# Sliding-window attention and a ternary feed-forward on one core: stage order and the attention's matmul layout are changed

## The chip, the cores and the metric

One core of one Trainium2 chip runs the whole program in one launch. The metric is the device time in microseconds (us). Engines: TensorE (PE, with its weight loads listed apart as PEld), VectorE (DVE), ScalarE (ACT), GpSimd (POOL) and SyncE (SP), which here only issues DMAs. Matmuls write PSUM: 8 banks of 512 fp32 columns on 128 partitions.

## The reference

```python
def ref(x, Wqkv, bqkv, Wout, bout, fast_b, w_fc, w_proj, u, v, gate):   # x: (1, 8192, 512) fp32
    xn = layernorm(x)
    q, k, v_ = split(xn @ Wqkv + bqkv)              # 16 heads of 32
    # a block of 128 queries sees its own block and both neighbours
    s = q @ kwin.T / sqrt(512);  s = where(|kpos - qpos| <= 128 and inside, s, -1e30)
    att = (softmax(s) @ vwin) @ Wout + bout
    h = bitlinear(xn, w_fc) + gate * (xn @ v.T @ fast_b.T @ u.T)        # 512 -> 2048
    ffn = bitlinear(relu(h) ** 2, w_proj)                               # 2048 -> 512, ternary weights
    return x + att + ffn
```

All is fp32. Both kernels reach that precision by splitting a value into a high part and a rest (`_hi`, `_lo`, type fp32r, which TensorE takes in one pass) and adding products of the parts.

## The kernel before, in words

`build` calls `attention`, which writes x + attention + bias to a DRAM buffer `partial`, and then `feed_forward`, which adds its result to `partial` and writes `out`. Each is a block of its own: one ends before the other begins. Every engine's order is written out by hand.

**Attention** (L192 to L1030) goes over 32 tiles of 256 tokens. A tile has 32 steps (`STEPS`), one for each pair of a head and a block of 128 queries. Four heads (32 channels each) make a chunk of 128 channels, so four chunks of 8 steps make a tile. A step:

- PE `scores` (L901): q and k are kept *stacked* in `stack`: 96 rows hold q_hi, q_lo, q_hi against k_hi, k_hi, k_lo, so one 96-row matmul gives the three products at once, 128 queries on partitions and 384 keys as columns. The stack is built by DMA from `qk_parts` (SP, `stack_qk`, L530: 12 DMAs of 64 KB a chunk).
- DVE `mask_scale_max` (L780) masks, scales and takes the row's maximum; ACT `exp` (L709) gives the probabilities in fp32.
- PE `transpose_probs` (L917): three 128x128 transposes turn them so that keys stand on partitions; ACT `pT_high` and DVE `pT_low` copy them out as two fp16 parts.
- PE `probs_times_values` (L938): for each of 3 key blocks two matmuls against `values`, which hold three bf16 parts of v and a column of ones. DVE `fold` (L807) adds the parts, POOL divides by the sum. The output goes back through PE ("riders", L923, 16 a tile with those of the next x) to be transposed.
- Between them on PE stand the *jobs* (`job_part`, L969), a quarter of one job in each step: q and k of a chunk (24 matmuls of 256 columns), v of a block and the output projection of a block (12 of 512 columns each). A tile has 4, 2 and 2 of them: 24 + 12 matmuls for each chunk.

**Feed-forward** (L1273) goes over 16 tiles of 512 tokens. `prepare_feed_forward` (L1037) quantises and transposes the weights. Then each of 16 steps of a tile has nine 512-column matmuls up and eight down; the next x is loaded, normalised and transposed beside them. PE is in order; SP loads x and `partial` and stores the result.

PE line numbers used below: L290 (project q, k), L300 (project v), L965 (project out), L913 (scores), L934 (transposes of the probabilities), L931 (riders), L954 and L956 (products with values), L188 (bias sum, fp32), L379 (first block's keys), L1225 (a scale spread by fp32 matmuls).

Of the kernel before, what the change touches and what calls it, by code (L numbers as in the profile page):

```python
# [32 lines left out]
VW = 1 + 3 * DH  # L33
# [9 lines left out]
def settle(eng, ticks):  # L43


    eng.sem_inc(ticks[eng.engine], 1)


def block_rows(dram, block):

    return dram[bass.ds(block * P, P), :]

# [13 lines left out]

def prepare_attention(nc, x, Wqkv, bqkv, Wout, bout, wqkv_hi, wqkv_lo, wout_hi, wout_lo, qk_bias, out_bias, ident,
                      minus_half, job_ps, xT_places):

    NX = len(xT_places)
    with ExitStack() as ctx:
        def sb(name, shape):  # L80
            return ctx.enter_context(nc.sbuf_tensor(name, shape, F32))

        def sem(name):
            return ctx.enter_context(nc.semaphore(name))

        stage = sb("w_stage", [P, DC, 3 * D])
        wout_raw = sb("wout_raw", [P, DC, D])
        v_bias = sb("v_bias", [P, DC])
        v_bias_wide = sb("v_bias_wide", [P, DC, P])
        bout_wide = sb("bout_wide", [P, D])  # L90
        x_in = sb("pro_x", [P, NX, D])
        bn = sb("pro_bn", [P, NX, 6])
        stats = sb("pro_stats", [P, NX, 4])
        bias_ps = ctx.enter_context(nc.psum_tensor("bias_ps", [P, D], F32))
        chunk_in = [sem(f"wqkv_chunk_in{k}") for k in range(DC)]
        wout_in, biases_in = sem("wout_in"), sem("biases_in")
        hi_done, lo_done = sem("w_hi_done"), sem("w_lo_done")
        wide_done, bias_summed = sem("v_bias_wide_done"), sem("bias_summed")
        zeroed, ident_done, half_set = sem("ident_zeroed"), sem("ident_done"), sem("pro_half_set")
        x_here = [sem(f"pro_x_here{b}") for b in range(NX)]  # L100
        ln_step = [sem(f"pro_ln_step{b}") for b in range(NX)]
        xn_done, x_turned, xT_hi_done, xT_done = (
            sem("pro_xn_done"), sem("pro_x_turned"), sem("pro_xT_hi_done"), sem("pro_xT_done"))
        block = ctx.enter_context(nc.Block())

        def four(ps):
            return ps.rearrange("p (c t) -> p c t", c=DC)

        @block.sync
        def _(sp):  # L110
            for b in range(NX):
                sp.dma_start(x_in[:, b, :], block_rows(x, b)).then_inc(x_here[b], 16)
            for k in range(DC):
                sp.dma_start(stage[:, k, :], Wqkv[k * P:(k + 1) * P, :]).then_inc(chunk_in[k], 16)
            sp.dma_start(wout_raw[:, :, :], Wout.rearrange("(c p) n -> p c n", p=P)).then_inc(wout_in, 16)

        @block.gpsimd
        def _(pool):
            identity_on_pool(pool, nc, ident, zeroed, ident_done)
            nc.gpsimd.memset(minus_half[:, :], -0.5).then_inc(half_set, 1)  # L120
            pool.wait_ge(half_set, 1)
            for b in range(NX):
                inverse_std(pool, nc, stats[:, b, :], minus_half, ln_step[b], 3)
            with nc.allow_non_contiguous_dma("a bias vector, once"):
                pool.dma_start(v_bias[:, :], bqkv[2 * D:3 * D].rearrange("(c p) -> p c", p=P)).then_inc(biases_in, 16)
                pool.dma_start(qk_bias[:, :], bqkv[0:2 * D].rearrange("(c p) -> p c", p=P)).then_inc(biases_in, 16)
# [67 lines left out]

# [1442 lines left out]
```

## Time and profile before

| | us |
|---|---|
| median of 3 runs (lowest, highest) | 2812.26 (2809.57, 2814.84) |
| the profiled execution: its own time | 2811.49 |
| its span, first to last instruction | 2809.7 |
| PE busy in the span | 2724.4 (97%) |
| mean granted clock | 0.985 of 2.4 GHz |

The profile is one execution. Starts of instructions are recorded; ends on PE are modelled, so the time that a matmul takes from its neighbours is the distance between two starts (the pitch), not its duration. `x3` in a row in order of time says that three equal instructions were merged. A granted clock of 1.00 is 2.4 GHz, 0.5 is 1.2 GHz.

### The profile page before, as it was taken

How to read it: one execution, taken by the hardware profiler on the slowest of the kernel's cores; microseconds unless marked ns; L12 is line 12 of the kernel's file. 1: busy time of each engine (PE TensorE's matmuls, PEld its weight loads, DVE VectorE, ACT ScalarE, POOL GpSimd, SP SyncE). 2: the span in 40 equal slices, each digit the busy share in tenths (PEclk: the TensorE clock that was granted, in tenths of full speed). 3: DMA queues.
4: the chain of work that ended last, by engine and by line, in shares of the span. 5: the costliest groups of instructions: out<-in, count | busy, mean ns of one | idle time of the engine just before them, and what ended most of it. 6: DMA issues, size and time to landing. Idle time of an engine off the chain costs nothing. (4 is left out here: it accounts for less than half of the span.)

```text
span 2809.7 us, 63144 instructions
## 1 busy us (share of the span) xinstructions
PE 2724.4 (97%) x20744; PEld 2393.8 (85%) x20744; DVE 2025.0 (72%) x5704; ACT 1713.7 (61%) x3745; POOL 640.1 (23%) x812
## 2 busy tenths in 40 slices
PE   6899999999999999999999976999999999999998
PEld 5899999999999999999999965888888888888887
DVE  4799999999999999999999966444444444444443
ACT  4678778787787877878778755333333333333332
POOL 3223333233332333333333220111111111111111
PEclk9999999999999999999999987999999999999999
DMA  3333333333333333333333333111111111111101
GB/s 113 92 97 92 99 95 97 96 91 99 96 92 100 94 98 96 94 97 94 99 96 95 98 90 135 44 50 49 45 49 45 49 45 45 45 45 45 45 30 45
DMA packets 176970, 219.39 MB, mean 78 GB/s; under 512 B 32112, under 2 KB 115280, under 8 KB 176192
## 3 DMA queue, kind: packets, MB, share of 16 engines
q1 hardware_dynamic: 175840, 215.31, 26.8%
q8 instruction: 142, 2.33, 0.4%
q0 software_dynamic: 864, 0.73, 0.1%
q14 instruction: 124, 1.02, 0.1%
HBM read 80.91 MB, written 33.55 MB: 41 GB/s over the span
## 5 line engine op out<-in xcount | busy, mean ns | idle before, releaser
L716 ACT ACTIVATE probs<-neg_scores,neg_max 128x384 f32<-128x384 f32 (+1 forms) x1024 | 631.0, 616 | 342.9 <-DVE neg_max L789 335.9
L789 DVE CUSTOM_DVE_ANT_0 neg_scores<-score_ps,mask 128x384 f32<-128x384 f32 (+1 forms) x1024 | 560.8, 548 | 106.0 <-PE score_ps L913 47.9
L1444 ACT ACTIVATE relu<-up_ps,fc_scale 128x512 f32<-128x512 f32 x256 | 176.4, 689 | 655.0 <-PE up_ps L1575 655.0
L800 DVE TENSOR_TENSOR pT_lo<-pT_ps,pT_hi 128x384 f16<-128x384 f32 (+1 forms) x1024 | 562.0, 549 | 13.1 <-ACT xT_hi L729 4.6
L1518 DVE SCALAR_TENSOR_TENSOR sq<-up_ps,relu 128x512 f32<-128x512 f32 x256 | 177.1, 692 | 533.3 <-ACT relu L1444 533.0
L934 PE MATMUL pT_ps<-ident,probs 128*128 128x128 f32 x3040 | 504.1, 274 | 16.7 <-ACT probs L716 13.5
L727 ACT CAST pT_hi<-pT_ps 128x384 f16<-128x384 f32 (+1 forms) x1024 | 470.0, 459 | 2.6 <-PE pT_ps L934 2.6
L913 PE MATMUL score_ps<-stack 96*128 96x128 f32 (+2 forms) x1536 | 447.2, 346 | 0.0
L934 PEld LDWEIGHTS pT_ps<-ident,probs 128*128 128x128 f32 x3040 | 364.4, 141 | 85.2 <-DVE oT_lo L804 13.1
L1585 PE MATMUL down_ps<-proj_T,sq_hi 128*128 128x512 f32 x1024 | 408.8, 399 | 0.3 <-DVE sq_lo L1501 0.2
L1587 PE MATMUL down_ps<-proj_T,sq_lo 128*128 128x512 f32 x1024 | 404.3, 395 | 0.0
L1571 PE MATMUL up_ps<-f_xT_hi,fc_T 128*128 128x512 f32 x1024 | 399.2, 390 | 1.4 <-DVE low L1489 1.4
L1573 PE MATMUL up_ps<-f_xT_lo,fc_T 128*128 128x512 f32 x1024 | 399.2, 390 | 0.0
L628 POOL TENSOR_TENSOR o_heads<-o_sum,o_rcp 128x128 f32<-128x128 f32 x256 | 102.8, 402 | 949.0 <-DVE o_sum L814 949.0
L290 PE MATMUL job_ps<-xT_hi,wqkv_hi 128*128 128x256 f32 x1024 | 295.2, 288 | 2.6 <-PEq L318 2.6
L954 PE MATMUL o_ps<-values,pT_hi 128*128 128x97 bf16 x3040 | 293.9, 207 | 0.5 <-DVE oT_lo L804 0.5
L290 PE MATMUL job_ps<-xT_hi,wqkv_lo 128*128 128x256 f32 x1024 | 288.2, 281 | 0.0
L290 PE MATMUL job_ps<-xT_lo,wqkv_hi 128*128 128x256 f32 x1024 | 287.6, 281 | 0.0
L956 PE MATMUL o_ps<-values,pT_lo 128*128 128x65 bf16 x3040 | 286.8, 193 | 0.0
L913 PEld LDWEIGHTS score_ps<-stack 96*128 96x128 f32 x1536 | 253.3, 192 | 0.1
L954 PEld LDWEIGHTS o_ps<-values,pT_hi 128*128 128x128 f16 x3040 | 250.3, 97 | 0.8 <-DVE oT_lo L804 0.6
L956 PEld LDWEIGHTS o_ps<-values,pT_lo 128*128 128x128 f16 x3040 | 237.6, 98 | 5.9
(165 smaller groups left out, 5189.4 us busy)
## 6 DMA issues: line engine op xcount, KB each, us to landing
stack<-qk_parts SPq DMA_DIRECT2D x1536, 64.0 KB, 2.1
x_in<-in_L_attn_x SPq DMA_DIRECT2D x64, 256.0 KB, 3.2
y<-in_L_attn_x SPq DMA_DIRECT2D x64, 256.0 KB, 2.8
partial<-y SPq DMA_DIRECT2D x64, 256.0 KB, 3.4
f_x_in<-in_L_attn_x SPq DMA_DIRECT2D x64, 256.0 KB, 2.7
part_in<-partial SPq DMA_DIRECT2D x64, 256.0 KB, 3.5
out<-f_y SPq DMA_DIRECT2D x64, 256.0 KB, 2.0
fc_in<-in_L_ffn_w_fc SPq DMA_DIRECT2D x16, 256.0 KB, 6.0
```

The source lines that it names most:

```text
L290: last = nc.tensor.matmul(out, w[:, k, col:col + P], a[:, k, par, :] if is_k else own_tokens(a, par, k), start=(n == 0), stop=(n == 3 * DC ...
L716: nc.scalar.activation(probs[:, r, cols], neg_scores[:, r, cols], ACT.Exp, bias=neg_max[:, s % 4:s % 4 + 1], scale=-1.0).then_inc(probs_do ...
L727: last = nc.scalar.copy(pT_hi[:, s % 4, cols], pT_ps[:, r, cols])
L789: nc.vector.tensor_tensor_reduce(out=neg_scores[:, r, cols], in0=score_ps[:, r, cols], in1=mask[:, cols], scale=-SCORE_SCALE, scalar=3e38, ...
L800: last = nc.vector.tensor_tensor(pT_lo[:, s % 4, cols], pT_ps[:, r, cols], pT_hi[:, s % 4, cols], ALU.subtract)
L913: last = nc.tensor.matmul(score_ps[:, s % 2, (w - b) * P:(w - b + count) * P], q_cols(par, c, h, b), keys[:, at:at + count * P], start=Tru ...
L934: last = nc.tensor.transpose(pT_ps[:, r, w * P:(w + 1) * P], probs[:, r, w * P:(w + 1) * P], ident[:, :])
L954: nc.tensor.matmul(o_ps[:, g % 2, col:col + VW], pT_hi[:, r, t], v, start=(w == w0), stop=False)
L956: last = nc.tensor.matmul(o_ps[:, g % 2, col:col + 1 + 2 * DH], pT_lo[:, r, t], v[:, 0:1 + 2 * DH], start=False, stop=(w == w1 - 1))
L1571: nc.tensor.matmul(up_ps[:, s % 2, :], fc_T[:, k, cols], xT_hi[:, par, k, :], start=(k == 0), stop=False)
L1585: nc.tensor.matmul(down_ps[:, b, :], sq_hi[:, s % 2, t], proj_T[:, s, :], start=(s == 0), stop=False)
L1587: last = nc.tensor.matmul(down_ps[:, b, :], sq_lo[:, s % 2, t], proj_T[:, s, :], start=False, stop=(s == FB - 1))
```

## The change

The feed-forward runs first. It takes the residual x in place of `partial` (`part_in <- x`) and writes `partial`; it also stores both parts of its transposed, normalised x to a new DRAM buffer `xT` (8 DMAs of 256 KB a tile of 512 tokens). Attention runs second, reads `xT` back (4 DMAs of 256 KB a tile of 256 tokens), adds `partial` and writes `out`. Its own layer norm, its transposes of x, the `stack` with its DMAs, the transposes of probabilities and outputs, and the fp16 and bf16 parts are gone.

Attention now goes by *slots*, 128 in all: one chunk of four heads of one tile of 256 queries (what 8 steps were). Heads use strips of the 128x128 array: `tile_position=(h * 32, 0)` puts a matmul with 32 rows on row strip h, `(0, h * 32)` one with 32 output columns on column strip h.

- `scores`: query-on-partition scores as before, but three matmuls of 32 rows for each head (hi·hi, lo·hi, hi·lo), the four heads one behind the other, each into its own PSUM bank. DVE takes from them only the maximum (`find_max`, 8 a slot). Where the keys wrap around in their ring of four blocks (every other tile), a run of 384 columns is cut in two.
- The maxima, as two fp32r parts in `shift_cols`, are turned by two matmuls (`turn_shift`) and copied by ACT to `shift_T`.
- `turned_scores` computes the scores a second time with keys on partitions, and adds minus the maximum (a matmul with `pick`) and the mask (16 bf16 matmuls on 32x32 tiles, `eye` by `turned_mask`) in PSUM. ACT takes the exponential straight into `pT`, fp32: 4 of 512 columns and 4 of 256 a slot.
- `probs_times_values`: fp32 matmuls, 32 output columns for each head, moving `pT`; once with the values and once with ones for the sums. DVE takes the reciprocal of 128x256 and multiplies.
- Banks: a ring of six (`RB`), 17 uses a slot, and two for the jobs and the products. The jobs are the same 24 + 12 matmuls a slot.

```diff
+def attention_stage(nc, Wqkv, bqkv, Wout, bout, xT_dram, partial, out):
+    RB = 6
+    USES = 4 * HC + 1
+            def scores(t, b):
+                ...
+                for w, key, count in key_runs(i, b):
+                    for pass_ in range(PASSES):
+                        q = q_lo if pass_ == 1 else q_hi
+                        keys = k_lo if pass_ == 2 else k_hi
+                        for h in range(HC):
+                            rows = slice(h * DH, (h + 1) * DH)
+                            last = nc.tensor.matmul(
+                                ring_ps[:, ring_bank(use + h), w * P:(w + count) * P], q[rows, c, place, :],
+                                keys[rows, c, key:key + count, :], start=(pass_ == 0), stop=(pass_ == PASSES - 1),
+                                tile_position=(h * DH, 0))
+            def turned_scores(t, edge):
+                ...
+                for h in range(HC):
+                    nc.tensor.matmul(ring_ps[:, ring_bank(use + h), cols], pick[rows, :], shift, start=True, stop=False,
+                                     tile_position=(h * DH, 0))
+                for h in range(HC):
+                    for g in range(HC):
+                        nc.tensor.matmul(strip[:, mask_places, :], eye[rows, :], turned_mask[rows, g, masks, :],
+                                         start=False, stop=False, tile_position=(h * DH, g * DH))
+                for key, out_cols, places in parts:
+                    for pass_ in range(PASSES):
+                        for h in range(HC):
+                            last = nc.tensor.matmul(
+                                ring_ps[:, ring_bank(use + h), out_cols], keys[rows, c, key, :], q[rows, c, places, :],
+                                start=False, stop=(key == parts[-1][0] and pass_ == PASSES - 1),
+                                tile_position=(h * DH, 0))
+            def probs_times_values(t):
+                ...
+                for sums in range(2):
+                    for n, (blk, cols, source) in enumerate(parts):    # 256, 256, 128, 128 columns
+                        for h in range(HC):
+                            v = ones[:, :] if sums else values[:, blk % VR, head * DH:(head + 1) * DH]
+                            last = nc.tensor.matmul(job_ps[strip, bank, out_], v, pT[:, t % 2, h, source],
+                                                    start=(n == 0), stop=(n == len(parts) - 1),
+                                                    tile_position=(0, h * DH))
+            for t in range(STEPS + 4):
+                if t < STEPS:
+                    scores(t, 0)
+                if 2 <= t < STEPS + 2:
+                    probs_times_values(t - 2)
+                run_a(t, 0)
+                if 1 <= t <= STEPS:
+                    turned_scores(t - 1, False)
+                run_a(t, 1)
+                if t < STEPS:
+                    scores(t, 1)
+                run_b(t, 0)
+                if 1 <= t <= STEPS:
+                    turned_scores(t - 1, True)
+                run_b(t, 1)
+                if t < STEPS:
+                    turn_shift(t)
...
+                nc.vector.reciprocal(o_rcp[:, :], job_ps[:, bank, T:2 * T]).then_inc(rcp_done, 1)
...
+                    nc.scalar.activation(pT[:, t % 2, h, 0:4 * P], ring_ps[:, bank, :], ACT.Exp,
+                                         scale=SCORE_SCALE).then_inc(exped, 1)
...
+            def store_xT(i, par):
+                for b in range(NB):
+                    sp.wait_ge(xT_done, NB * i + b + 1)
+                    for low, xT in enumerate((xT_hi, xT_lo)):
+                        sp.dma_start(xT_rows(xT_dram, NB * i + b, low),
+                                     xT[:, par, :, b * P:(b + 1) * P].bitcast(F32)).then_inc(xT_stored[b], 16)
...
             def xT_high(i, par, b):
                 act.wait_ge(x_turned, NB * i + b + 1)
+                wait(act, xT_stored[b], 32 * (i - 1))
...
 def prepare_attention(...):        # POOL now also builds pick, ones, eye and turned_mask
+                    nc.gpsimd.affine_select(out=raw_mask[rows, :, n, :], in_=raw_mask[rows, :, n, :],
+                                            compare_op=ALU.is_ge, fill=NEG, base=0,
+                                            pattern=[[-sign * DH, HC], [sign, P]], channel_multiplier=-sign
+                                            ).then_inc(consts_set, 1)
...
 def feed_forward(nc, x, partial, fast_b, w_fc, w_proj, u, v, gate, out):
+    xT_dram = nc.dram_tensor("xT", [2 * x.shape[0], x.shape[1]], F32, kind="Internal").ap()
+    feed_forward_stage(nc, x, fast_b, w_fc, w_proj, u, v, gate, xT_dram, partial)
+    attention_stage(nc, *HELD["attention"], xT_dram, partial, out)
```

## Rows read from the trace of the kernel before

**Rows 1.** the page, engines busy; then granted clock in 40 slices
```profile
PE 2724.4 (97%) x20744; PEld 2393.8 (85%) x20744; DVE 2025.0 (72%) x5704; ACT 1713.7 (61%) x3745; POOL 640.1 (23%) x812
...
PEclk9999999999999999999999987999999999999999
```

**Rows 2.** stretches: length, busy PE, PEld, DVE, ACT, POOL, clock, DMA share, GB/s
```profile
0.00:1668.00 1668.00, 1623.35 (x15833) 1499.76 (x15834) 1498.71 (x4690) 1281.24 (x3012) 511.84 (x673) 0.99 0.36 96
1668.00:1744.00 76.00, 43.87 (x202) 32.53 (x201) 45.59 (x123) 43.37 (x86) 8.43 (x15) 0.66 0.47 162
1744.00:2800.00 1056.00, 1055.73 (x4707) 860.58 (x4708) 478.23 (x887) 389.06 (x647) 114.91 (x120) 1.00 0.13 44
```

**Rows 3.** stretches within the attention: steady state, then its run-out
```profile
400.00:1600.00 1200.00, 1198.22 (x11858) 1111.73 (x11855) 1113.94 (x3493) 954.41 (x2250) 374.34 (x480) 1.00 0.36 96
1645.00:1660.00 15.00, 10.97 (x99) 9.13 (x96) 11.67 (x42) 9.25 (x24) 1.20 (x3) 0.82 0.16 55
```

**Rows 4.** groups, 400 to 1600 us: count, busy us, mean ns, idle before
```profile
L934 PE MATMUL pT_ps<-ident,probs 128*128 128x128 f32 x2295 | 376.6, 273 | 1.8 <-ACT probs L716 0.9
...
L954 PE MATMUL o_ps<-values,pT_hi 128*128 128x97 bf16 x2296 | 220.5, 207 | 0.0
...
L814 DVE TENSOR_REDUCE o_sum<-o_ps 128x128 f32<-128x384 f32 x192 | 101.0, 526 | 0.0
```

**Rows 5.** order of time, PE, 1000 to 1004 us: start, duration, instruction
```profile
999.75 0.28 PE L290 MATMUL job_ps<-xT_hi,wqkv_hi 128*128 128x256 f32 x1
999.87 0.28 PE L290 MATMUL job_ps<-xT_lo,wqkv_hi 128*128 128x256 f32 x1
...
1000.57 0.49 PE L934 MATMUL pT_ps<-ident,probs 128*128 128x128 f32 x3
1000.81 0.48 PE L913 MATMUL score_ps<-stack 96*128 96x128 f32 x2
...
1002.27 0.21 PE L954 MATMUL o_ps<-values,pT_hi 128*128 128x97 bf16 x1
...
1002.69 0.19 PE L956 MATMUL o_ps<-values,pT_lo 128*128 128x65 bf16 x1
1002.72 0.42 PE L913 MATMUL score_ps<-stack 96*128 96x256 f32 x2
1002.98 0.44 PE L300 MATMUL job_ps<-wqkv_hi,xT_hi 128*128 128x512 f32 x1
1003.26 0.40 PE L300 MATMUL job_ps<-wqkv_hi,xT_lo 128*128 128x512 f32 x1
1003.49 0.41 PE L300 MATMUL job_ps<-wqkv_lo,xT_hi 128*128 128x512 f32 x1
```

**Rows 6.** order of time, PE: the fp32 matmuls at L1225
```profile
1724.39 1.06 PE L1225 MATMUL scale_ps<-diagonal,ones 128*128 128x128 f32 x8
```

**Rows 7.** order of time, PEld: weight loads of fp32 matmuls
```profile
25.91 0.19 PEld L188 LDWEIGHTS bias_ps<-wout_raw,v_bias_wide 128*128 128x128 f32 x1 [0.38 <-issue]
26.34 0.19 PEld L188 LDWEIGHTS bias_ps<-wout_raw,v_bias_wide 128*128 128x128 f32 x1 [0.24 <-issue]
```

**Rows 8.** order of time, PEld: weight loads of 128-column fp32r matmuls
```profile
31.51 0.19 PEld L379 LDWEIGHTS job_ps<-xT_hi,wqkv_hi 128*128 128x128 f32 x1
31.62 0.19 PEld L379 LDWEIGHTS job_ps<-xT_lo,wqkv_hi 128*128 128x128 f32 x1
```

**Rows 9.** VectorE and ScalarE groups in 400 to 1600 us
```profile
L716 ACT ACTIVATE probs<-neg_scores,neg_max 128x384 f32<-128x384 f32 x766 | 474.7, 620 | 246.0 <-DVE neg_max L789 240.6
...
L789 DVE CUSTOM_DVE_ANT_0 neg_scores<-score_ps,mask 128x384 f32<-128x384 f32 x765 | 422.1, 552 | 74.0 <-PE score_ps L913 29.4 <-ACT probs L716 25.2 <-issue 0.8
...
L789 DVE DVE_READ_ACCUMULATOR2_ANT neg_max<- 128x1 f32 x765 | 63.1, 82 | 0.0
...
L813 DVE RECIPROCAL o_rcp<-o_ps 128x4 f32<-128x4 f32 x192 | 33.7, 176 | 2.3
```

**Rows 10.** VectorE groups in 1690 to 1730 us
```profile
L1137 DVE RECIPROCAL inv_scale<-scale 128x1 f32<-128x1 f32 x12 | 1.9, 156 | 0.0
```

More of the change, by code:

```diff
@@ L32 @@
 ROUND = 1.5 * 2.0 ** 23
-VW = 1 + 3 * DH
 def wait(eng, sem, value):
@@ L46, in settle, with xT_rows @@
     eng.sem_inc(ticks[eng.engine], 1)
+    eng.sem_inc(ticks[eng.engine], 1)
 def block_rows(dram, block):
     return dram[bass.ds(block * P, P), :]
+def xT_rows(dram, block, low):
+    return dram[bass.ds((2 * block + low) * P, P), :].rearrange("p (k t) -> p k t", k=DC)
 def identity_on_pool(pool, nc, ident, zeroed, ready):
@@ L1270, in _, with feed_forward_stage @@
                 nc.scalar.copy(low_out[:, n * D:(n + 1) * D], turn_ps[0:3 * DH, n, :]).then_inc(u_copied, 1)
-def feed_forward(nc, x, partial, fast_b, w_fc, w_proj, u, v, gate, out):
+def feed_forward_stage(nc, x, fast_b, w_fc, w_proj, u, v, gate, xT_dram, partial):
     F = w_fc.shape[0]
@@ L1334, in feed_forward @@
         stored = [sem(f"stored{b}") for b in range(NB)]
+        xT_stored = [sem(f"xT_stored{b}") for b in range(NB)]
         block = ctx.enter_context(nc.Block())
@@ L1370, in _ @@
                 sp.sem_inc(stored[b], 16)
+            def store_xT(i, par):
+                for b in range(NB):
+                    sp.wait_ge(xT_done, NB * i + b + 1)
+                    settle(sp, ticks)
+                    for low, xT in enumerate((xT_hi, xT_lo)):
+                        sp.dma_start(xT_rows(xT_dram, NB * i + b, low),
+                                     xT[:, par, :, b * P:(b + 1) * P].bitcast(F32)).then_inc(xT_stored[b], 16)
+            store_xT(0, 0)
             def tile(i, par):
@@ L1378, in tile @@
                         settle(sp, ticks)
-                        sp.dma_start(block_rows(out, NB * (i - 1) + b), y[:, b, :]).then_inc(stored[b], 16)
+                        sp.dma_start(block_rows(partial, NB * (i - 1) + b), y[:, b, :]).then_inc(stored[b], 16)
                 for b in range(NB):
-                    sp.dma_start(part_in[:, b, :], block_rows(partial, NB * i + b)).then_inc(part_here[b], 16)
+                    sp.dma_start(part_in[:, b, :], block_rows(x, NB * i + b)).then_inc(part_here[b], 16)
+                if not is_last(i):
+                    store_xT(i + 1, 1 - par)
             tiles(sp, tile)
@@ L1385, in _ @@
                 sp.wait_ge(y_done, NB * (NT - 1) + b + 1)
-                sp.dma_start(block_rows(out, NB * (NT - 1) + b), y[:, b, :]).then_inc(stored[b], 16)
+                sp.dma_start(block_rows(partial, NB * (NT - 1) + b), y[:, b, :]).then_inc(stored[b], 16)
             for b in range(NB):
                 sp.wait_ge(stored[b], 16 * (NT + 1))
+                sp.wait_ge(xT_stored[b], 32 * NT)
         @block.gpsimd
@@ L1613, with attention, feed_forward @@
+HELD = {}
+def attention(nc, x, Wqkv, bqkv, Wout, bout, partial):
+    HELD["attention"] = (Wqkv, bqkv, Wout, bout)
+def feed_forward(nc, x, partial, fast_b, w_fc, w_proj, u, v, gate, out):
+    xT_dram = nc.dram_tensor("xT", [2 * x.shape[0], x.shape[1]], F32, kind="Internal").ap()
+    feed_forward_stage(nc, x, fast_b, w_fc, w_proj, u, v, gate, xT_dram, partial)
+    attention_stage(nc, *HELD["attention"], xT_dram, partial, out)
 _INS = ["L0_attn_x", "L0_attn_Wqkv", "L0_attn_bqkv", "L0_attn_Wout", "L0_attn_bout", "L0_ffn_fast_b", "L0_ffn_w_fc",
```

1372 lines of the change are left out of this document (578 added, 794 removed).

## The prediction

> **What bounds the kernel now.** I read the page's busy line first, then the stretches, then TensorE's rows in order of time. PE is busy 97% of the span and its clock is at its upper level nearly throughout [rows 1]. The attention takes 1668 us, the feed-forward's preparation and first transposes 76 us, its steady part 1056 us with PE never idle [rows 2]. In the attention's steady part PE is busy for 1198 of 1200 us, DVE for 1114 [rows 3]; the transposes, PE's first to wait for anybody, wait 1.8 us in all [rows 4]. DVE's fold L814 runs 192 times there, 8 a tile, so 24 tiles: 50.0 us a tile, **12.5 us a slot** (a chunk of four heads, 8 steps). PE's order sets the end in both stages, and the change is worth what it does to PE's 12.5 us.
>
> What fills them, by pitches [rows 5]: the q and k matmuls follow at 0.12 (24 a slot: 2.8 us), the 512-column ones at 0.23 (12: 2.8 us), the three transposes of a step take 0.24 (24 and 4 riders: 2.3 us), twelve value products 0.45 (48: 1.8 us), a step's score matmuls 0.26 (2.1 us). Sum 11.8; 0.7 us are handovers.
>
> **What stays.** The feed-forward's PE order is the same. New there are 8 stores of xT a tile of 66 us, 2 MB or 32 GB/s beside the 44 that it moves now, while the attention moves 96 [rows 2]: hidden, on SP's queue behind loads that are one tile early; were they late, the wait would be ACT's copy of a tile two back. Cost 0 (bounds 0 and 10 us). The attention's preparation loses layer norm and gains some 25 small POOL operations beside the same weight loads; its first slot still waits for 36 + 24 + 48 matmuls, and x now comes from DRAM. Its run-out stands at the kernel's end and the feed-forward's before the attention. I set all of this to 0, bounds -10 and +30 us. So T = 2811.5 (the profiled execution, 0.8 under the median) + 128 x (new slot - 12.5).
>
> **The jobs** are the same: 5.6 us a slot.
>
> **What goes:** stacked scores, transposes, riders, bf16 products, 6.2 us a slot, and DVE's and ACT's copies, which were beside PE anyway.
>
> **What comes, on PE.** No row of the trace has strips of the array, so each term is bounded from both sides: all strips at once, or one after the other.
>
> 1. *Products with values and ones.* An fp32 matmul is two records: the four at L1225 are x8 in the trace [rows 6]. A record takes 0.43 us for 512 columns [rows 7], two cycles of 2.4 GHz a column, and 0.11 us for 128, from (1.06 - 0.27) / 7 [rows 6]. So a 256-column head product is 2 x 0.21 = 0.43 us. A slot has 2 x (256 + 256 + 128 + 128) columns for each of four heads: 2.6 us if four strips run at once, 10.2 us if none do. I take **5.1**: matmuls start in program order [rows 5], and the two records of one head stand next to each other on the same strip. The second must wait for the first, and the next head's first starts behind it. Only a second record and the next head's first can overlap, so half of the serial cost stays.
> 2. *Row-strip groups of four heads.* Scores: two directions x 3 passes of 384 columns, or 256 and 128 where keys wrap: 6 or 12 groups, 9 on average. Turned scores: 7 groups (one of 512, six of 256), then 7 (one of 256, six of 128). At 0.457 ns a column (0.117/256) and a weight load of 128 columns at 0.11 [rows 8] as the floor of each strip, all at once is 1.2 + 0.9 + 0.8 = 2.9 us. But each group is four load-and-matmul pairs, and the fastest pairs in the trace come at 0.038 us (eleven from 1002.27 to 1002.69 [rows 5], of 97 and 65 columns), 0.15 a group: 1.4 + 1.1 + 1.0 = **3.5**, which I take. If loads of different strips don't overlap, 92 loads x 0.11 = 10.1 us; with nothing overlapping 11.
> 3. *Masks.* 32 small bf16 matmuls of 256 columns: 0.2 us all at once, 3.7 one by one; at the issue pitch 32 x 0.038 = **1.2**.
> 4. *Turning the maxima:* 2 x 0.11 = **0.2**.
>
> Sum: 5.6 + 5.1 + 3.5 + 1.2 + 0.2 = **15.6 us a slot**, 3.1 more than now.
>
> **The other engines** don't reach that. DVE: 8 maxima x (0.55 + 0.08) = 5.0; a reciprocal costs 156 ns at one column and 176 at four [rows 9, 10], 6.7 ns a column, so 1.9 us for 256; the rest (product 0.4, q and k rests 1.0, the split 0.4, half an output 0.3) makes 9.0. ACT: eight exponentials, 4 x 0.73 + 4 x 0.51 (0.62 at 384 columns [rows 9]), and some 2 us of copies: 7. PE waits for ring banks: the turned scores need two of the four banks just scored, 1.3 us of DVE, behind 5.1 us of products; the second scores need two exponentials, 1.5 us, behind 1.4 us of job. Such waits cost tenths at most: 0, upper bound 0.5 us a slot. Queued behind a waiting matmul is all of PE, the jobs too; here a pause of 0.5 us meets DVE and ACT with half of their time free.
>
> The sum is 128 x 3.1 = 397 us: **3210 us**.
>
> **A rule that would add to it.** By the Trainium skill (TensorEngine Tiling (Array Packing), Key Properties) "changing tiling mode (not just tile) drains the TensorE". In this trace nothing shows it: the 97-column products follow transposes and 96-row scores follow them without a gap of over 0.1 us [rows 5]. My sum goes without it.
>
> **Rivals.**
> - *Strips really run four at once, issue costs nothing* (0.20): 5.6 + 2.6 + 2.9 + 0.4 + 0.2 = 11.7 us, **2710**. For it: PE's whole argument is then columns, and a 384-column group hides its issue. Against it: the two records of an fp32 product must start out of order. The skill (TensorE: Matmul & The Clock Gate, Packing small matmuls) says that matmuls on different strips start about 4 ns apart, and also that they start in strict order; the first half would give this case, both together my forecast.
> - *Four at once for the fp32 products, pairs at 0.038* (0.10): 13.1 us, **2890**: slower still.
> - *Each change of strip shape drains PE* (0.13): a slot changes shape some 13 times (scores, products, job, turned scores around the masks, job, and so on). A drain is the part of a matmul behind its pitch, 0.40 - 0.23 = 0.17 us [rows 5]: 2.2 us a slot, **3490**. This is what the rule above would do.
> - *Weight loads of different row strips go one by one* (0.13): 5.6 + 5.1 + 10.1 + 1.2 + 0.2 = 22.2 us, **4050**. For it: loads are the floor of a 128-column matmul now [rows 8]. Against it: a strip's load touches other rows of the array.
> - *No overlap at all, so that strips don't do what they say* (0.04): 5.6 + 10.2 + 11 + 3.7 + 0.2 = 30.7, **5140**.
>
> My forecast has 0.40. The faster case turns on one point: with everything else ideal the slot is 9.1 + products, so products must cost under 3.4 us, which half overlap (5.1) excludes.
>
> A clock at the lower level is no case of its own: in the run-out PE was busy 11 of 15 us and the clock 0.82 [rows 3], but a PE-bound slot has no such pauses.
>
> **Range.** The forecast's own is 3050 to 3350 (a third less or all of the bank waits, issue at 0.025 to 0.04). With the rivals at 2710, 2890 and 3490 the range is 2690 to 3700; 4050 and 5140 (0.17) are left out. Executions agree within 0.2%, so that is what can be told from no change: faster 0.21, within 0.2% 0.01, slower 0.78.
>
> **What would show it.** The jobs' pitches unchanged at 0.12 and 0.23. For the products: starts of four heads' records; 1.71 us for four heads at 256 columns is serial, 0.85 to 1.07 my half, 0.43 full overlap. For the row strips: the time from one pass's first head to the next pass's, 0.15 to 0.18, against 0.44 for serial loads. Stretches of the feed-forward as before. PE near 100% busy in the attention, DVE near 60%, ACT near 45%. Wrong it would be if the products of a slot took under 3.4 us, if PE waited for DVE's maxima or for exponentials by over 0.5 us a slot, or if the granted clock fell in the steady part.

## The result, and the profile after

The changed kernel takes 2987.8 us (median; 2986.8 to 2991.4) against 2813.6 us for the kernel before on the same chip: a ratio of 1.063, 95% interval 1.061 to 1.064. I had forecast 3210 us. Slower it is, by 174 us where I had said 397.

The page after, busy engines and the granted clock, beside [rows 1]:

```profile
PE 2899.6 (97%) x33680; PEld 2280.8 (76%) x33680; DVE 1512.4 (51%) x3905; ACT 1068.2 (36%) x2341; POOL 325.7 (11%) x367
...
PEclk6999999999999996999999999999999999999999
```

TensorE is as busy as before (97%), with 1.6 times as many matmul records (33680 for 20744). The stretches of the changed kernel: feed-forward's preparation, its steady part, the attention's preparation in two pieces, and the attention in steady state (columns as in [rows 2]):

```profile
0.00:76.00 76.00, 47.32 (x205) 35.89 (x206) 46.28 (x124) 44.80 (x87) 6.44 (x17) 0.69 0.53 182
76.00:1132.00 1056.00, 1052.50 (x4693) 857.60 (x4691) 478.23 (x890) 387.65 (x646) 117.22 (x123) 1.00 0.24 74
1132.00:1160.00 28.00, 6.59 (x32) 1.38 (x32) 8.61 (x6) 7.78 (x5) 22.60 (x37) 0.53 0.55 193
1160.00:1190.00 30.00, 16.59 (x70) 15.49 (x71) 3.06 (x6) 1.73 (x5) 2.66 (x1) 0.54 0.44 123
...
1300.00:2700.00 1400.00, 1394.71 (x22644) 1078.11 (x22644) 766.57 (x2251) 492.16 (x1250) 138.21 (x150) 1.00 0.13 40
```

The edges of these stretches are chosen, not found. From the first to the last matmul of the feed-forward's tiles it is 1058.6 us, where it was 1057.2, now with 74 GB/s where it had 44 [rows 2]: its eight stores a tile are hidden. Its preparation, up to that first matmul, takes 69.8 us from the start of the span; before, it took 72.4 us from the attention's last matmul. In the attention's steady part PE is busy for 1394.7 of 1400 us at a granted clock of 1.00. VectorE, which stood at 93% [rows 3], is at 55%. So what has grown is the work on TensorE itself. The slot is read from VectorE's reciprocal, one a slot; the row gives count, shortest, median and longest in ns, and first and last start:

```profile
L1135 DVE RECIPROCAL o_rcp<-job_ps x128: 1756/1758/1759, 1218.2 to 2977.7; 128x256 f32<-128x256 f32 x128
```

(2977.7 - 1218.2) / 127 = **13.85 us a slot**, against 12.5. 128 x 1.35 = 173 us, of the 180 us between the two profiled spans (2989.6 and 2809.7). The other 7 lie outside the slots, in the preparations and the run-out, which I had set to 0.

One slot in order of time on PE (start, duration, instruction). xcount is what the view puts in one row; x4 is the four heads of a row-strip pass:

```profile
2000.87 0.28 PE L1203 MATMUL job_ps<-xT_hi,wqkv_lo 128*128 128x256 f32 x1
2001.07 0.51 PE L1300 MATMUL ring_ps<-shift_T,pick 32*128 32x512 f32 x4
2001.51 0.33 PE L1306 MATMUL ring_ps<-turned_mask,eye 32*32 32x256 bf16 x16
2001.77 0.39 PE L1314 MATMUL ring_ps<-q_hi,k_hi 32*128 32x256 f32 x4
2001.99 0.29 PE L1314 MATMUL ring_ps<-q_lo,k_hi 32*128 32x256 f32 x4
2002.11 0.29 PE L1314 MATMUL ring_ps<-q_hi,k_lo 32*128 32x256 f32 x4
...
2002.47 0.28 PE L1314 MATMUL ring_ps<-q_hi,k_lo 32*128 32x256 f32 x4
2002.68 0.39 PE L1203 MATMUL job_ps<-xT_hi,wqkv_hi 128*128 128x256 f32 x1
2002.90 0.28 PE L1203 MATMUL job_ps<-xT_lo,wqkv_hi 128*128 128x256 f32 x1
2003.02 0.28 PE L1203 MATMUL job_ps<-xT_hi,wqkv_lo 128*128 128x256 f32 x1
...
2010.56 0.28 PE L1270 MATMUL ring_ps<-k_lo,q_hi 32*128 32x128 f32 x4
2010.77 1.51 PE L1351 MATMUL job_ps<-pT,values 128*32 128x256 f32 x32
2012.09 1.48 PE L1351 MATMUL job_ps<-pT,ones_strip 128*32 128x256 f32 x32
2013.51 0.38 PE L1203 MATMUL job_ps<-xT_hi,wqkv_hi 128*128 128x256 f32 x1
```

What to see there:

- The jobs' pitches are unchanged: 0.12 us (2002.90 to 2003.02).
- *Products.* 32 records with values and 32 with ones, from 2010.77 to 2013.51: 2.74 us. Four heads' first records start 7 ns apart (2010.767, .774, .781, .787), their second ones 0.24 us later: all four strips run at once.
- *Row strips.* A pass of four heads takes 0.12 us (2001.99 to 2002.11), as long as one matmul of 256 columns on the whole array.
- *Edges.* Wherever the tile shape changes, the distance is too long. The last 256-column job matmul is followed after 0.20 us (2000.87 to 2001.07) where 0.12 is its pitch. The maxima's 512 columns, pitch 0.23, take 0.44 until the masks. The masks take 0.26 where a job matmul of as many columns takes 0.12, the first pass of turned scores 0.22 (2001.77 to 2001.99), the last one 0.21 (2002.47 to 2002.68), and the first job matmul behind it 0.22. Each change of shape costs about 0.1 us on the last group ahead of it and 0.1 on the first behind it, and there are 13 a slot. A change of operands in one shape costs nothing: the last output job is followed by the turning of the maxima, also on the whole array, after 0.24 us (2009.43 to 2009.67), its pitch being 0.23.
- *Weight loads at an edge.* Within a shape a load starts ahead of its own matmul, 0.12 us here (2000.75 for the matmul at 2000.87). Across a change it starts only together with it (2001.07 for 2001.07). In the 1400 us, no load starts between the last matmul before a change and the first behind it in 1275 of 1300 changes.

```profile
2000.75 0.19 PEld L1203 LDWEIGHTS job_ps<-xT_hi,wqkv_lo 128*128 128x128 f32 x1
2001.07 0.19 PEld L1300 LDWEIGHTS ring_ps<-shift_T,pick 32*128 32x128 f32 x4
```

VectorE and ScalarE in steady state, beside my prices of 0.55, 0.73 and 1.9 us; the idle time in front of them shows that they wait for PE, and not the other way:

```profile
L1116 DVE CUSTOM_DVE_ANT_0 masked_scores<-ring_ps,mask 128x384 bf16<-128x384 f32 x800 | 398.3, 554 | 473.2 <-PE ring_ps L1270 473.2
...
L1051 ACT ACTIVATE pT<-ring_ps 128x512 f32<-128x512 f32 x400 | 206.6, 604 | 626.9 <-PE ring_ps L1314 626.9
L1135 DVE RECIPROCAL o_rcp<-job_ps 128x256 f32<-128x256 f32 x101 | 177.5, 1758 | 82.7 <-PE job_ps L1351 82.7
```

PE's own waits in the same 1400 us are this one row:

```profile
PE job_ps L1351 <- issue: 5.3, 25, 0.3
```

### The profile page after: what moved, and what is told of

Read it like the earlier page. It is cut to its first block, busy times and chain, and to the rows that moved or that the text cites. A ratio compares the mean times of both kernels' runs of the same rounds, so it can differ in the third digit from the quotient of the medians.

```text
span 2989.6 us, 79871 instructions
## 1 busy us (share of the span) xinstructions
PE 2899.6 (97%) x33680; PEld 2280.8 (76%) x33680; DVE 1512.4 (51%) x3905; ACT 1068.2 (36%) x2341; POOL 325.7 (11%) x367
## 4 chain that ended last, share of the span: by engine, by line
PE 60%; issue 0%; DVE 0%; ACT 0%; DMA 0%; SPq 0%; POOL 0%; POOLq 0%; ACTq 0%
PE job_ps L1203 14%; PE job_ps L1351 12%; PE ring_ps L1314 7%; PE job_ps L1212 7%; PE ring_ps L1270 7%; PE job_ps L1223 7%; PE ring_ps L1300 3%; PE ring_ps L1306 2%; PE ring_ps L1327 1%; PE job_ps L1363 0%; DMA xT_lo<-xT 0%; SPq L984 0%; DVE masked_scores L1116 0%; ACT pT L1051 0%; DVE o_rcp L1135 0%
## 5 line engine op out<-in xcount | busy, mean ns | idle before, releaser
L1116 DVE CUSTOM_DVE_ANT_0 masked_scores<-ring_ps,mask 128x384 bf16<-128x384 f32 (+1 forms) x1024 | 505.5, 550 | 599.0 <-PE ring_ps L1270 599.0
L1051 ACT ACTIVATE pT<-ring_ps 128x512 f32<-128x512 f32 x512 | 264.4, 604 | 794.2 <-PE ring_ps L1314 794.2
L1135 DVE RECIPROCAL o_rcp<-job_ps 128x256 f32<-128x256 f32 x128 | 225.0, 1758 | 112.2 <-PE job_ps L1351 112.2
L623 PEld LDWEIGHTS up_ps<-f_xT_hi,fc_T 128*128 128x128 f32 x1024 | 192.8, 188 | 44.2 <-DVE low L541 2.2
L637 PEld LDWEIGHTS down_ps<-proj_T,sq_hi 128*128 128x128 f32 x1024 | 193.4, 189 | 42.8 <-DVE sq_lo L553 1.1
L639 PEld LDWEIGHTS down_ps<-proj_T,sq_lo 128*128 128x128 f32 x1024 | 193.0, 188 | 43.1
L625 PEld LDWEIGHTS up_ps<-f_xT_lo,fc_T 128*128 128x128 f32 x1024 | 192.8, 188 | 42.6
L1351 PE MATMUL job_ps<-pT,values 128*32 128x256 f32 (+1 forms) x4032 | 193.0, 332 | 6.6 <-issue 6.6
L1203 PEld LDWEIGHTS job_ps<-xT_hi,wqkv_lo 128*128 128x128 f32 x1024 | 193.0, 188 | 0.0
L1203 PEld LDWEIGHTS job_ps<-xT_lo,wqkv_hi 128*128 128x128 f32 x1024 | 192.8, 188 | 0.1
```

The source lines that it names most:

```text
L623: nc.tensor.matmul(up_ps[:, s % 2, :], fc_T[:, k, cols], xT_hi[:, par, k, :], start=(k == 0), stop=False)
L625: nc.tensor.matmul(up_ps[:, s % 2, :], fc_T[:, k, cols], xT_lo[:, par, k, :], start=False, stop=False)
L637: nc.tensor.matmul(down_ps[:, b, :], sq_hi[:, s % 2, t], proj_T[:, s, :], start=(s == 0), stop=False)
L639: last = nc.tensor.matmul(down_ps[:, b, :], sq_lo[:, s % 2, t], proj_T[:, s, :], start=False, stop=(s == FB - 1))
L1051: nc.scalar.activation(pT[:, t % 2, h, 0:4 * P], ring_ps[:, bank, :], ACT.Exp, scale=SCORE_SCALE).then_inc(exped, 1)
L1116: nc.vector.tensor_tensor_reduce(out=masked_scores[:, b * HC + h, cols], in0=ring_ps[:, bank, cols], in1=mask[:, cols], scale=-1.0, scalar ...
```

## Experiments

All are edits of the changed kernel. A slot's time is read from the reciprocal's starts, as above. The kernels ran on four chips; each ratio is to the kernel before on the same chip, which took 2811 us (2809 for the last kernel). The diffs are shortened, some to lines in words.

### The order of the heads in the products

```diff
-for sums in range(2):
-    for n, (blk, cols, source) in enumerate(parts):
-        for h in range(HC):
+for sums in range(2):
+    for h in range(HC):
+        for n, (blk, cols, source) in enumerate(parts):
```

The wait for the edge exponentials, which stood ahead of the third key block, now stands ahead of all the products. It isn't the cause of what follows: PE's waits come to 3.8 us in 1400, against 5.3 before the edit.

> The value and ones products take the heads in the outer loop and the key blocks in the inner one: the same matmuls, but all of one strip stand next to each other. Theory A (matmuls start strictly in program order, and one whose strip is busy holds up every later one): the four strips no longer run at once, the products go from 2.7 us a slot to between 8 and 10.2, +5.5 to +7.5 us a slot, so 3690 to 3950 us. Theory B (each strip has work of its own waiting, and a later strip's matmul passes one whose strip is busy): nothing changes, 2988 us within 15. Theory C (it can look ahead, but only over a few matmuls): in between; a strip has 8 records in a row there. The slot's period and the starts of the four heads' records show which.

Measured: 3599 us, ratio 1.280 (1.278 to 1.282), 18.66 us a slot, +4.80. PE in order of time:

```profile
1999.83 1.60 PE L1350 MATMUL job_ps<-pT,values 128*32 128x256 f32 x11
2001.16 0.40 PE L1350 MATMUL job_ps<-pT,ones_strip 128*32 128x256 f32 x1
2001.27 0.38 PE L1350 MATMUL job_ps<-pT,values 128*32 128x128 f32 x2
2001.40 0.38 PE L1350 MATMUL job_ps<-pT,ones_strip 128*32 128x256 f32 x1
...
2001.62 3.71 PE L1350 MATMUL job_ps<-pT,ones_strip 128*32 128x256 f32 x30
```

Products with ones of one head stand among products with values of another (2001.16 to 2001.62): strips do overlap, but late. The block takes 7.5 us instead of 2.74. The starts of the records, read one by one (columns: start, column count):

```
head 0:  2016.303 256   .543 256   .759 256   .975 256   2017.191 128   .300 128   .409 128   .518 128
head 1:  2017.196 256   .436 256   .652 256   .868 256   2018.084 128   ...
head 2:  2018.090 256   ...
```

Head 1 begins 5 ns after head 0's fifth record of eight starts, head 2 again 6 ns after head 1's fifth. So it looks as if three records of a strip can wait behind the one that starts, and the matmuls of other strips pass them, while a further one holds up everything behind it in program order. Eight such blocks: 7 offsets of 0.89 us are 6.25, and the last block 1.30: 7.55, as measured. Neither theory A nor theory B but C.

### The same for the row strips

```diff
-for w, key, count in key_runs(i, b):
-    for pass_ in range(PASSES):
-        for h in range(HC):
+for h in range(HC):
+    for w, key, count in key_runs(i, b):
+        for pass_ in range(PASSES):
```

(and likewise in `turned_scores`.)

> Same edit for the row strips: heads outside, passes inside, in the scores of both directions and in the turned scores. The slot has 21 groups of four matmuls that take 2.9 us when the four strips run at once. Theory A (in program order, a busy strip holds up all): up to four times that less the overlap of the ends, +5 to +8 us a slot, 3630 to 4000 us. Theory B (a strip's matmul passes one that waits for another strip): 2988 us within 15. Theory C (look-ahead over a few only): in between. The bank of head 0 is then finished earlier than the others; maxima and exponentials are beside PE anyway, so that is worth 0.

Measured: 3347 us, ratio 1.191 (1.189 to 1.193), 16.62 us a slot, +2.77. The turned scores of a main block in order of time, three matmuls of the first head, and then a row that merges the second head's first (2008.163) with the first head's fourth (2008.276):

```profile
2007.82 0.38 PE L1314 MATMUL ring_ps<-q_hi,k_hi 32*128 32x256 f32 x1
2008.04 0.28 PE L1314 MATMUL ring_ps<-q_lo,k_hi 32*128 32x256 f32 x1
2008.16 0.28 PE L1314 MATMUL ring_ps<-q_hi,k_lo 32*128 32x256 f32 x1
2008.16 0.39 PE L1314 MATMUL ring_ps<-q_hi,k_hi 32*128 32x256 f32 x2
```

A head has six records here. The next head's first starts 6 ns after the third (2008.157 and 2008.163): again three are left waiting, and a matmul starts ahead of one that stands before it in program order. Where a head has three records, as in the scores whose keys don't wrap, all four heads start within 30 ns (2054.305 to 2054.335), and the order of the heads costs next to nothing: the group takes 0.75 us to the next one, against 0.73. That is why the price is 2.77 us and not theory A's 5 to 8. Two kinds of matmul, fp32 in column strips and fp32r in row strips, give the same number, three records.

### Two matmuls a head before the next head

```diff
-for n, (blk, cols, source) in enumerate(parts):
-    for h in range(HC):
+for pair in range(0, len(parts), 2):
+    for h, n in ((h, n) for h in range(HC) for n in range(pair, min(pair + 2, len(parts)))):
+        blk, cols, source = parts[n]
```

> Between the changed kernel and the one with the heads outermost: the products take the key blocks two at a time, so each head issues two fp32 matmuls (four records) before the next head's. Theory R (a strip takes a few records ahead: the records of the heads-outer kernels show the next head's first starting 6 ns after the strip before it has three records left, fp32 or fp32r; matmuls are handed out in program order into that room): four records fit, so nothing changes, 2988 us within 10. Theory M (room for one record behind the running one): each pair of matmuls delays the next strip by two records of 0.216 us, +1.2 us for each of the four pairs of 256 or 128 columns together about +3.5 us a slot, 3430. What I had predicted (no room at all) would make it slower still.

Measured: 2997 us, ratio 1.066 (1.065 to 1.068), 13.93 us a slot: +0.08, where theory M asked for 3.5. Four records fit. The values pass takes 1.33 us, in the changed kernel 1.32:

```profile
2011.44 1.54 PE L1352 MATMUL job_ps<-pT,values 128*32 128x256 f32 x32
2012.77 1.55 PE L1352 MATMUL job_ps<-pT,ones_strip 128*32 128x256 f32 x32
```

The four heads' first records are now 13 ns apart instead of 7 (2011.441 to 2011.481). When the fourth head starts, three records of each of the other three are waiting, nine in all. So the room is each strip's own, and not one of three for all strips together, which the kernel with the heads outermost in the products can't tell apart.

### Is the overlap real, and is TensorE the bound?

```diff
-for sums in range(2):
+for sums in (0, 1, 1):
```

> The products with ones are done twice (the second pass overwrites the first with the same sums): 16 fp32 matmuls more a slot, 32 records. Theory F (four strips at once, and TensorE is the bound): the 12 records of the values pass took 1.37 us, so +1.33 to +1.37 us a slot, +170 to +175 us, 3160. Theory H (my half overlap, hidden somewhere in the trace): +2.55 us a slot, +326 us, 3314. Theory W (a wait for VectorE or ScalarE fills part of the slot): less than +100 us.

Measured: 3156 us, ratio 1.122 (1.121 to 1.124), 15.19 us a slot, +1.33. Theory F; half overlap would have given twice that. (A pass has 32 records, not the 12 of the expectation.) The 64 records with ones take 2.74 us, 1.37 a pass:

```profile
2006.08 1.51 PE L1351 MATMUL job_ps<-pT,values 128*32 128x256 f32 x32 [0.27 <-issue]
2007.38 2.81 PE L1351 MATMUL job_ps<-pT,ones_strip 128*32 128x256 f32 x64
2010.12 0.39 PE L1203 MATMUL job_ps<-xT_hi,wqkv_hi 128*128 128x256 f32 x1
```

### More changes of shape

```diff
-for h in range(HC): masks of head h
-turned scores, passes 1 to 6
+for h in range(2): masks of head h
+turned scores, pass 1
+for h in range(2, 4): masks of head h
+turned scores, passes 2 to 6
```

> The 16 mask matmuls before the turned scores are done in two batches of eight, with the first pass of the turned scores (four row-strip matmuls) between them: the same instructions in another order. It adds two changes of tile shape to each of the two turned-score groups, four to a slot. Theory D (each change of shape drains TensorE; 0.195 us a change, from the stretched distances in the changed kernel's trace): +0.78 us a slot, +100 us, 3088 (within 25). Theory N (no price on a change; the 1.2 us a slot that my accounting lacks lie elsewhere, in issue for example): 2988 within 10.

Measured: 3091 us, ratio 1.100 (1.098 to 1.101), 14.63 us a slot, +0.77. The instructions are the same: theory D. Each group has its own two edges now:

```profile
2001.54 0.30 PE L1307 MATMUL ring_ps<-turned_mask,eye 32*32 32x256 bf16 x8
2001.77 0.39 PE L1316 MATMUL ring_ps<-q_hi,k_hi 32*128 32x256 f32 x4
2002.09 0.30 PE L1307 MATMUL ring_ps<-turned_mask,eye 32*32 32x256 bf16 x8
2002.32 0.39 PE L1316 MATMUL ring_ps<-q_lo,k_hi 32*128 32x256 f32 x4
2002.54 0.28 PE L1316 MATMUL ring_ps<-q_hi,k_lo 32*128 32x256 f32 x4
```

Eight masks take 0.23 us (2001.54 to 2001.77), and sixteen took 0.26: a group of masks costs its two edges and hardly its matmuls. Pass 1 between the masks takes 0.32 (2001.77 to 2002.09), with a change on both sides, and pass 2 0.22, with one behind it; without any it is 0.12.

### Fewer changes of shape

Edge masks ahead of the maxima, so that the maxima and the turned scores stand together:

```diff
-nc.tensor.matmul(ring_ps[...], pick[rows, :], shift, start=True, ...)
+if edge: masks_of(True)                 # the masks open the bank
+nc.tensor.matmul(ring_ps[...], pick[rows, :], shift, start=not edge, ...)
+if not edge: masks_of(False)
```

> In the turned scores of the edge blocks the masks come ahead of the matmuls that add the maxima, so that those stand next to the turned scores, which have the same shape: job, masks, maxima, turned scores instead of job, maxima, masks, maxima's shape again. One change of tile shape fewer a slot, same instructions. Theory D (0.195 us a change): -25 us, 2963 (within 8). Theory N: 2988 within 4.

Measured: 2961 us, ratio 1.054 (1.052 to 1.055), 13.64 us a slot, -0.22. On top of it, the q and k job in one piece:

```diff
-run_a(t, 0)
 if 1 <= t <= STEPS: turned_scores(t - 1, False)
+run_a(t, 0)
 run_a(t, 1)
```

> On top of the kernel with the edge masks first: the turned scores of the main blocks come straight after the products and before the q and k job, whose two halves then stand together. The same instructions, two changes of tile shape fewer (job to maxima, turned scores to job). Theory D: -0.39 us a slot, 2961 - 50 = 2911. Rival: the turned scores now need the maxima of two of the four banks just scored, with only the products between; if those take longer than the products' 2.7 us, TensorE waits and the gain is lost, 2950 to 3000.

Measured: 2940 us, ratio 1.046 (1.044 to 1.047), 13.47 us a slot, -0.17. I had miscounted: products, job, maxima become products, maxima, so one change goes, not two; for one change theory D asks for -0.2. PE didn't wait for the maxima. And on top of that, the main masks last:

```diff
-if not edge: masks_of(False)
 for key, out_cols, places in parts: ...      # turned scores
+if not edge: last = masks_of(False)
```

> On top of the kernel with the jobs together (2940 us; my count of its changes was wrong: it saves one, not two, since the products then meet the row strips directly; it has 11 a slot against 12 and 13): the masks of the main blocks come last in their group, between the turned scores and the job, so that the maxima and the turned scores, which have one shape, stand together. Same instructions, 10 changes a slot. Theory D, at the 0.17 to 0.21 us that the last two removals gave: 2913 to 2919. Theory N: 2940.

Measured: 2913 us, ratio 1.036 (1.035 to 1.038), 13.31 us a slot, -0.16. Five kernels with the same instructions now stand in one line:

| changes of shape a slot | us a slot | time, us |
|---|---|---|
| 17 | 14.63 | 3091 |
| 13 (the changed kernel) | 13.85 | 2988 |
| 12 | 13.64 | 2961 |
| 11 | 13.47 | 2940 |
| 10 | 13.31 | 2913 |

The slope is (14.63 - 13.31) / 7 = **0.19 us a change**. By that slope, carried on below the 10 that were tried, 13 of them are an estimated 2.5 us a slot, 316 us, more than the 174 us that the changed kernel lost, and without them the slot would take 11.4 us.

### Fewer columns

What I tried next is in the products. The three key blocks' probabilities are added before the sum over keys is taken, so that one matmul of 256 columns a head replaces four. First with GpSimd doing both adds, on the kernel with 12 changes:

```diff
+nc.gpsimd.tensor_tensor(p_sum, pT[main block 0], pT[main block 1], ALU.add)
+nc.gpsimd.tensor_tensor(p_sum[edge cols], p_sum[edge cols], pT[edge cols], ALU.add)
-ones products of all four parts
+nc.tensor.matmul(job_ps[strip, bank, T:2 * T], ones, p_sum[:, t % 2, h, :], start=True, stop=True, ...)
```

> The kernel with the edge masks first, and the probabilities of the three key blocks added beforehand, both adds on GpSimd; the one ones product a head stands behind the turned scores of the main blocks, some 4 us after the value products. By pitches: -0.94 us a slot of products, and one change of tile shape more (turned scores, sums, job in place of turned scores, job), +0.2: 2961 - 120 + 25 = 2866. Rival: GpSimd's two adds of 1024 columns (2.4 us each in the last profile) end too late and TensorE waits: 2900 to 2960.

Measured: 2881 us, ratio 1.024 (1.022 to 1.026), 13.02 us a slot: -0.62 against the 12-change kernel, where the sum said -0.74. Then with the jobs together, the sums next to the value products, and VectorE adding the edges (11 changes):

> What the measurements point to, all at once: edge masks first; jobs together; and the sums from probabilities added beforehand over the three key blocks (GpSimd adds the two main blocks, VectorE the edge ones), so that one fp32 matmul of 256 columns a head replaces four, next to the value products. By the pitches: -27 (measured), -50 (two changes), -0.94 us a slot for 1.37 - 0.43 us of ones products, -120: 2791 us, 0.7% below the kernel before. Rival: the sums come late (GpSimd 2.5 us for 1024 columns by its 1.28 us for 512, then VectorE behind the edge exponentials), TensorE waits in front of them, and the 120 us are lost in part: 2820 to 2900, slower than before.

Measured: 2847 us, ratio 1.013 (1.012 to 1.015), 12.73 us a slot. The 2791 had my miscount in it; by the kernel with 11 changes it is 13.47 - 0.94 = 12.53. Of the missing 0.2 us about 0.1 is in my 0.94, which is 1.37 - 0.43: the group of ones products, from its first start to the next group's, goes from 1.41 us (11 changes, old sums) to 0.55 where nothing waits, since its edge stays, and that is 0.86. The other 0.1 is a wait, though not the rival's: the same distance is 0.65 us here on average. PE's waits in the 1400 us, PE between the ones products and the maxima, and VectorE ahead of that:

```profile
PE ring_ps L1330 <- DVE neg_max L1127: 5.2, 27, 0.2
...
2006.50 0.61 PE L1386 MATMUL job_ps<-p_sum,ones_strip 128*32 128x256 f32 x8
2007.18 0.51 PE L1330 MATMUL ring_ps<-shift_T,pick 32*128 32x512 f32 x4
```

```profile
2004.87 1.22 DVE L1176 TENSOR_TENSOR p_sum<-p_sum,pT 128x1024 f32<-128x1024 f32 x1
2006.00 0.55 DVE L1127 CUSTOM_DVE_ANT_0 masked_scores<-ring_ps,mask 128x384 bf16<-128x384 f32 x1
...
2006.95 0.08 DVE L1127 DVE_READ_ACCUMULATOR2_ANT neg_max<- 128x1 f32 x1
```

The ones products start in time (2006.50, behind 1.33 us of values). But the edge add, 1.22 us, stands in front of VectorE's maxima, whose second one frees the second bank at 2007.03; the maxima's matmuls start at 2007.18. With the add shared between VectorE and GpSimd, and the main masks last (ten changes):

```diff
-dve: p_sum[:, 0:4, edge] += pT[:, 0:4, edge]
+dve: p_sum[:, 0:2, edge] += pT[:, 0:2, edge]
+pool: p_sum[:, 2:4, edge] += pT[:, 2:4, edge]
```

> The last combination (2847 us), with the main masks last as well, and the edge add shared: VectorE adds the edge probabilities of two heads, GpSimd those of the other two. Ten changes a slot. In the last profile TensorE stood 0.25 us in front of the maxima's matmuls, waiting for VectorE's second maximum, behind its add of 1.22 us; with half of the add that goes, -0.2 us a slot, 25 us. The change of shape gives 25 more: 2797 (within 12), 0.5% below the kernel before. Rival: GpSimd's half, 1.2 us behind the last exponential and slowed by VectorE, is late for the ones products instead: 2810 to 2830, no better than before.

Measured: 2815 us, ratio 1.0009 (1.0000 to 1.0018), 12.44 us a slot; by 13.31 - 0.94 it would be 12.37, with 0.86 it is 12.45. Level with the kernel before. One of PE's waits is left, once in four slots; the two rows of ScalarE and the one of PE show where it is:

```profile
PE job_ps L1389 <- issue: 6.0, 28, 0.3
```

```profile
2012.63 0.37 ACT L1058 CAST shift_T<-ring_ps 128x256 fp32r<-128x256 f32 x1 [0.55 <-PE ring_ps L1365]
2012.90 0.59 ACT L1064 COPY values<-job_ps 128x512 f32<-128x512 f32 x1
```

```profile
2013.59 0.64 PE L1389 MATMUL job_ps<-pT,values 128*32 128x256 f32 x8 [0.16 <-issue]
```

The first product of a new tile needs the v block that ScalarE copies at 2012.90, behind the turned maxima's copy at 2012.63. Turning these two round:

```diff
-copy_shift(t - 1)
 if b and b[0] == "v": take_v(...)
+copy_shift(t - 1)
```

> The ten-change kernel (2815 us, as long as the kernel before) with one edit on ScalarE: v is copied out of its job's bank before the turned maxima are, and not after. In the last profile the products wait 0.2 us in front of their first matmul 28 times in 1400 us, once in each four slots, with 'issue' as the cause; the copy of v (0.59 us) ended at that point. If the wait is for that copy: 32 x 0.2 = 6 us less, 2808, level with or 0.1% below the kernel before. If it is something else: no change.

Measured: **2803 us** against 2809, ratio 0.9977 (0.9968 to 0.9986), 12.39 us a slot: below the kernel before by 0.2%, little, but with the interval clear of 1. The edit takes 0.05 us off the slot, 6 us in all, as I expected, and 5.2 us off the profiled span (2806.8 to 2801.6). The medians, each taken beside its own kernel before, differ by nearly 10; the ten-change kernel's executions lie between 2808.6 and 2819.2, so I don't count the rest. PE is never idle in the steady state:

```profile
1300.00:2700.00 1400.00, 1400.00 (x22675) 1106.35 (x22668) 935.05 (x2634) 562.84 (x1402) 612.94 (x392) 1.00 0.15 44
```

## Why the prediction was wrong

Bound and place were right, and so was the direction, though by errors that offset each other. The size was not: 13.85 us a slot where I had 15.6. By my own steps:

- *What stays.* Right: the feed-forward's steady part is unchanged within 1.4 us, the stores are hidden, and what is outside the slots is 7 us, within -10 to +30. The jobs' pitches, and with them their 5.6 us, are unchanged.
- **Step 1, products: the step that failed.** I took 5.1 us; they take 2.6 of matmuls (8 records of 0.216 and 8 of 0.109), in a block of 2.74, under the 3.4 that I had named as the sign of being wrong. My argument was that the second record of a head must wait for the first, and that the next head's first starts behind it in program order. The first half holds. The second doesn't: the second record waits in its strip, where there is room for three, and the next head passes it. With the heads outermost, where the room doesn't do, my picture comes true, and costs 4.8 us a slot.
- *Step 2, row strips.* I took 3.5, issue-bound at 0.038 us a pair. They take some 2.9, my bound for all at once (4.1 us from start to start, of which the twelve edges of six groups are 1.2 at 0.1 each): the distance of pairs in [rows 5] was that of 97 and 65 columns on the whole array. At 0.457 ns a column that is 0.044 and 0.030 us, 0.037 on average, so columns and not issue. Heads of different strips start 3 to 4 ns apart there (2001.072 to 2001.082).
- *Step 3, masks.* I took 1.2 at the same issue pitch; 16 start within 50 ns, 3.3 ns apart, and both groups together take 0.51 us, of which their four edges are 0.4. Same mistake; my bound of 0.2 us holds.
- *Step 4:* 0.2, right. *Bank waits:* 0, right; PE's waits are 5.3 us in 1400. *VectorE and ScalarE:* the slot's VectorE work is 766.6 / 101 = 7.6 us for my 9.0, in part since the maxima's second instruction (0.08 us) overlaps the next one; the reciprocal takes 1.76 for 1.9, the large exponential 0.60 for 0.73.
- *The drain.* I wrote it at 0 and gave it to a rival, with 13 changes at 0.17 us, 2.2 us a slot. It is 0.19 us, 2.5 us a slot. My evidence against it was a row of the kernel before in which products with 97 columns follow transposes, and scores with 96 rows follow those, without a gap [rows 5]. Those are other operand sizes, but no other tiling: nothing in that kernel used strips, so its trace couldn't speak on this. The rule of the Trainium skill that I quoted (TensorEngine Tiling (Array Packing), Key Properties) is borne out in this much, that a change has a price: the five kernels agree on 0.19 us. That the array is drained is not shown by itself; the trace shows that the first load behind a change doesn't start early.

So the rivals of four strips at once (11.7 us) and of the drain (2.2 us) were both true, and together they are 13.9 us, 2990, beside 2988 measured. I had listed them as alternatives, and added the drain only to my own sum. Three terms too large by 4.1 us (2.5, 0.6, 1.0) were in part made up for by one that was too small by 2.5 (together they give 14.0; the slot is 13.85). The net error of 1.75 us a slot hides errors of more than that on both sides: that the direction came out right was luck. With the three terms right and the drain still at 0 the sum is 11.5 us, 2680: faster than before. With the drain added and the three terms as they were, it is 3490. Of the Trainium skill's two sentences on start order (TensorE: Matmul & The Clock Gate, Packing small matmuls), the some 4 ns between strips are borne out (3.3 for masks, 7 for fp32 products); strict start order is not: in the kernel with the heads outermost in the scores a matmul starts at 2008.163 ahead of one before it in program order, at 2008.276. With the heads innermost the matmuls of one shape do start in program order, and only second records of fp32 ones come late (2011.007, behind the fourth head's first at 2010.787).

What stays open: whether the room is three records whatever their size (I saw 128 and 256 columns, fp32 and fp32r, and nothing of bf16), and what TensorE does in the 0.19 us of a change, whether it empties the array or fetches weights late. GpSimd's form of the sums was 0.12 us a slot above its sum; 0.08 of that is the 0.94 that should be 0.86, and the rest is open.

## What to carry to other kernels

Work in strips pays in full only if two things are in order. Put the strips in the innermost loop, or at least give none more than four records in a row, since a full strip holds up all others (+0.08 us a slot for four records in a row, +4.80 for eight). And count the places where the tile shape changes, at 0.2 us each: group what has one shape, put a mask first or last rather than in the middle, and never interleave small groups of two shapes. When rivals are about different mechanisms, add them up as well: the combination is a case of its own.

## What the hardware showed that I had not expected

- A strip has room for three records behind the one that starts: the next strip started 5 to 6 ns after the one that left three behind, with eight fp32 records and with six fp32r ones; nine records waited at once in three strips.
- A change of tile shape costs 0.19 us, half before and half behind it, and the first weight load behind it isn't started ahead of its matmul, also between strips of 32 rows and tiles of 32x32. A group of 8 masks took 0.23 us and one of 16 took 0.26.
- Order alone is worth 178 us between kernels with the same instructions (17 and 10 changes), and 611 us with the heads outermost in the products.
- GpSimd's add of 512 columns took 1.80 us beside VectorE's add of 0.69 us for as many, at the same time and on the same buffers (2012.2 in the ten-change kernel; 1.54 and 0.85 on average); an add of 512 columns in the changed kernel took it 1.28, one of 1024 columns in its own form of the sums 2.38.
